# Decoder layers stepped in pairs: two token tiles and two head pairs per cycle instead of one

## What is computed

```python
for i in range(DEPTH):                       # 6
    x = attn_layer(shift_tokens(x), Wqkv[i], q_scale[i], k_scale[i], Wo[i]) + x
    x = ffn_layer(shift_tokens(x), ln_g[i], ln_b[i], W1[i], b1[i], W2[i], b2[i]) + x

def attn_layer(x, Wqkv, qs, ksc, Wo):        # 16 heads of 64
    q, k, v = split heads of x @ Wqkv
    q, k = l2norm(q) * qs, l2norm(k) * ksc   # then both rotated by position
    out = local_attention(q, k, v)           # windows of 32 tokens, each sees itself and the one before
    return out @ Wo

def ffn_layer(x, g, bln, W1, b1, W2, b2):
    a, gate = split((layernorm(x) * g + bln) @ W1 + b1)
    return a * gelu(gate) @ W2 + b2
```

## Time and profile before

| | us |
|---|---|
| median of three runs | 4019.3 (4017.72 to 4019.72) |
| profiled execution | 4023.95 |
| its span, first to last instruction | 4022.2 |
| TensorE busy | 3794.5 (94%) |
| ScalarE busy | 3434.5 (85%) |
| VectorE busy | 3330.3 (83%) |
| GpSimd busy | 2815.3 (70%) |
| mean granted clock of TensorE | 0.983 |

### The profile page before, as it was taken

How to read it: one execution, slowest core, us unless ns; L and a number is a source line. 1 busy time by engine, 2 the same in 40 slices (tenths; PEclk the granted TensorE clock), 3 DMA queues, 4 the chain that set the end, 5 groups by cost and what they waited for, 6 DMA issues and landing times. The chain is left out here.

```text
span 4022.2 us, 139579 instructions
## 1 busy us (share of the span) xinstructions
PE 3794.5 (94%) x47336; PEld 3111.3 (77%) x47336; DVE 3330.3 (83%) x8535; ACT 3434.5 (85%) x11691; POOL 2815.3 (70%) x2443
## 2 busy tenths in 40 slices
PE   7999989999999999999999999999999999999993
PEld 4666668888888888888888888887888888888883
DVE  7888878888888888888878888888888888888883
ACT  7888868888888889888888888889888888888881
POOL 0111178878878787887877878787887878878781
PEclk9999999999999999999999999999999999999996
DMA  2000011111111111111111111111111111111111
GB/s 93 5 17 4 7 30 50 35 27 33 31 48 37 29 32 27 37 50 31 32 28 34 49 33 34 27 33 32 49 36 28 32 27 37 30 30 32 28 27 45
DMA packets 202441, 133.42 MB, mean 33 GB/s; under 512 B 123792, under 2 KB 195856, under 8 KB 200720
## 3 DMA queue, kind: packets, MB, share of 16 engines
q1 hardware_dynamic: 201744, 124.48, 12.0%
HBM read 25.84 MB, written 4.19 MB: 7 GB/s over the span
## 5 line engine op out<-in xcount | busy, mean ns | idle before, releaser
L1050 POOL TENSOR_TENSOR a_rn<-a_ssqc,a_minus_half 128x8 f32<-128x8 f32 x768 | 1273.6, 1658 | 621.7 <-DVE a_ssqc L1170 605.3
L993 ACT ACTIVATE a_E<-bank,a_negmax 128x96 f32<-128x96 f32 x3072 | 1008.1, 351 | 39.3 <-DVE a_negmax L1129 36.6
L1042 POOL TENSOR_TENSOR a_r<-a_u,a_rn 128x512 f32<-128x512 f32 x768 | 809.9, 1055 | 0.7
L1058 POOL TENSOR_TENSOR a_PN<-a_E,a_erec 128x384 f32<-128x384 f32 x768 | 659.0, 858 | 55.1 <-DVE a_erec L1177 55.1
L1020 ACT ACTIVATE a_QK<-bank 128x512 f32<-128x512 f32 x768 | 459.3, 598 | 261.7 <-PE bank L902 260.6
L993 ACT ACTIVATION_READ_ACCUMULATOR a_E<-bank,a_negmax 128x1 f32 x3072 | 669.3, 218 | 0.0
L1129 DVE TENSOR_REDUCE a_negmax<-bank 128x4 f32<-128x384 f32 x768 | 425.5, 554 | 255.8 <-PE bank L919 252.6
L1011 ACT ACTIVATE a_PT<-bank 128x512 f32<-128x512 f32 x768 | 467.6, 609 | 82.2 <-PE bank L892 76.8
L1154 DVE TENSOR_TENSOR a_u<-a_u,a_v 128x512 f32<-128x512 f32 x768 | 523.9, 682 | 6.0 <-issue 1.2
L1147 DVE TENSOR_TENSOR a_v<-bank,a_rot_s 128x512 f32<-128x512 f32 x768 | 524.1, 682 | 0.0
L1140 DVE TENSOR_TENSOR a_u<-bank,a_rot_c 128x512 f32<-128x512 f32 x768 | 522.6, 681 | 0.0
(11 more groups left out here) (139 smaller groups left out, 8701.6 us busy)
## 6 DMA issues: line engine op xcount, KB each, us to landing
a_V_even<-a_V_odd SPq DMA_DIRECT2D x768, 64.0 KB, 1.9
a_V_even<-a_V_odd SPq DMA_DIRECT2D x576, 32.0 KB, 1.9
w_qkv<-in_qkv SPq DMA_DIRECT2D x6, 1536.0 KB, 6.3
a_x_sh<-X SPq DMA_DIRECT2D x48, 128.0 KB
a_f_sh<-X SPq DMA_DIRECT2D x48, 128.0 KB
a_x_sh<-X SPq DMA_DIRECT2D x48, 127.0 KB
a_f_sh<-X SPq DMA_DIRECT2D x48, 127.0 KB
w_out<-in_wo SPq DMA_DIRECT2D x20, 128.0 KB, 2.3
```

Source lines behind the costliest of these rows:

```text
L993: ins = act.activation(E[:, s.par, i, :], p_s[:, i % 2, i // 2 * KW:(i // 2 + 1) * KW], ACT.Exp, bias=negmax[:, s.par, i:i + 1], accum_out ...
L1042: pool.tensor_tensor(heads(r[:, a.par, :]), heads(u[:, a.par, :]), rn[:, a.par, :].unsqueeze(2).to_broadcast([P, 2 * HG, DH]), ALU.mult).t ...
L1050: pool.tensor_tensor(rn[:, a.par, :], ssqc[:, a.par, :], minus_half[:, :], ALU.pow).then_inc(S["rn"], 1)
L1058: pool.tensor_tensor(PN[:, s.par, :, :].rearrange("p i (b k) -> p i b k", b=2)[:, :, :, 0:KW], windows(E[:, s.par, :, :]), windows(erec[:, ...
```

## The change

The layer loop goes over `n` and eight cycles `p` now; a cycle takes two token tiles (`mm` 0 and 1) and both head pairs (`hp` 0 and 1).

- **TensorE**: the tiled matmuls of both head pairs stand one behind the other (16 outputs, then 8 masks, then 16 logits). Projections of the two tiles stand apart, with the rest of the work between them.
- **Joint instructions**: one copy of values and one of outputs for both (512 columns instead of 256), one maximum, one sum of squares, one clamp, one rotation sum (1024 columns), one power (16 columns). Squares, rotation products, exponentials, reciprocals, probabilities and unit scaling stay apart.
- **PSUM**: the logits of both head pairs fill two banks. Transposes go to two banks, `p_ta` and `p_tb`, and the feed-forward results share these two in place of `p_f`.
- **Lags**, in cycles: transposes 2, logits 4, probabilities 6, outputs and output projection 7 (before, in steps: 2, 5, 7, 8, 9).
- **Feed-forward**: still two iterations behind, at other places: statistics in cycle 0, normalisation in 1, turn in 2, gates in 3 and 4, GELU and down projection in 5, values in 6 and 7. The load of `a_f_sh` for batch `n - 2` is issued in cycle 0, the load of the next x in cycle 1.
- **Weights**: the raw query, key and value weights of the next layer are loaded in groups to two buffers (`raw`) instead of whole.

The diff, cut to its core:

```diff
-LAG_T, LAG_S, LAG_PT, LAG_O, LAG_Y = 2, 5, 7, 8, 9
-J_TURN, J_GATE, J_GELU, J_VALUE, J_X = 1, 2, 5, 7, 11
-J_LOAD, J_X_LOAD, J_STATS, J_POWER, J_NORM = 9, 12, 13, 14, 15
+NP = STEPS // 2
+LAG_T, LAG_S, LAG_PT, LAG_O, LAG_Y = 2, 4, 6, 7, 7
+P_BIAS, P_NORM, P_TURN, P_GATE, P_GATES, P_GELU, P_VALUES, P_X = 1, 1, 2, 3, 4, 5, 6, 7
...
         for n in range(NI + 3):
-            for j in range(STEPS):
-                step(n, j)
+            for p in range(NP):
+                cycle(n, p)
...
@@ SyncE @@
+            def move_values(a):
+                name = f"v_moved{a.half}_{a.layer}"
+                m = 2 * a.half
+                sp.wait_ge(S["v_out"], a.k + 1)
+                ge(sp, S[name], moved.get(name, 0))
+                sp.dma_start(V_even[WIN:KW, a.g, m:m + 2, :], V_odd[0:64, a.g, m:m + 2, :]).then_inc(S[name], 16)
...
+            def cycle(n, p):
+                a = pair_at(n, p, 0)
                 if a:
...
+                    move_values(a)
+
+                f = n - 2
+                if p == 0 and 0 <= f < NI:
+                    sp.wait_ge(S["x_out"], f + 1)
+                    ge(sp, S["normed"], f)
+                    shifted_loads(sp, f_sh, X, f % NB, S["f_loaded"])
+                if p == 1 and 1 <= n < NI - 1:
+                    sp.wait_ge(S["xt"], n + 1)
+                    ge(sp, S["f_out"], n + 2 - NB)
+                    shifted_loads(sp, x_sh, X, (n + 1) % NB, S["x_loaded"])
...
@@ TensorE @@
+            def cycle(n, p):
+                project(n, p, 0)
+                transpose_probs(n, p, 1)
+                outputs(n, p)
+                logits(n, p)
+                transpose_qk(n, p, 0)
+                if p == P_BIAS:
+                    shifts(n)
+                if p == P_GATE:
+                    up(n, p, 0, 0, p_tb)
+                if p == P_X and n + 1 < NI:
+                    transpose_x(n + 1)
+                project(n, p, 1)
+                if p == P_TURN:
+                    turn(n)
+                if p == P_GATES:
+                    up(n, p, 1, 0, p_tb)
+                if p == P_VALUES:
+                    up(n, p, 0, 1, p_tb)
+                if p == P_X:
+                    up(n, p, 2, 1, p_ta)
+                values(n, p)
+                if p == P_GATES:
+                    up(n, p, 2, 0, p_ta)
+                if p == P_VALUES:
+                    up(n, p, 1, 1, p_ta)
+                transpose_qk(n, p, 1)
+                output_projection(n, p)
+                transpose_probs(n, p, 0)
+                if p == P_GELU:
+                    down(n)
...
@@ ScalarE @@
+            def cycle(n, p):
+                probs(n, p, 1)
+                outputs(n, p)
+                squares(n, p, 0)
+                queries_and_keys(n, p, 0)
...
+                squares(n, p, 1)
...
+                exps(n, p, 0, 0)
+                exps(n, p, 0, 1)
...
+                queries_and_keys(n, p, 1)
+                values(n, p)
+                probs(n, p, 0)
+                exps(n, p, 1, 0)
+                exps(n, p, 1, 1)
+                if p == P_GELU:
+                    gelu(n)
...
@@ GpSimd @@
+            def cycle(n, p):
+                power(n, p)
+                probs(n, p, 0)
+                probs(n, p, 1)
+                units(n, p, 1)
+                units(n, p, 0)
...
@@ VectorE @@
+            def stats(n):
+                f = n - 2
+                if 0 <= f < NI:
+                    dve.wait_ge(S["f_loaded"], 48 * (f + 1))
+                    statistics(dve, f_sh, st, ag, ve, S["stats"], S["aggr"], S["var"], f)
...
+            def cycle(n, p):
+                if p == P_X:
+                    residual(n)
+                maxima(n, p)
...
+                cosines(n, p, 0)
...
+                sines(n, p, 0)
+                norms(n, p)
+                if p == P_BIAS:
+                    split_up(n)
+                    biases(n)
+                cosines(n, p, 1)
+                clamp(n, p)
+                sines(n, p, 1)
+                if p == P_NORM:
+                    norm(n)
+                reciprocals(n, p, 0)
+                if p == 0:
+                    stats(n)
+                if p == P_GELU:
+                    feed_forward_out(n)
+                reciprocals(n, p, 1)
+                add(n, p)
+                split_qkv(n, p)
```

More of the change, by code:

```diff
@@ L786, in feed_forward, with up @@
+            def up(n, p, c, part, bank):
                 f = n - 2
[L787 to L793 removed]
@@ new lines, in outputs @@
+            def outputs(n, p):
+                a, o = pair_at(n, p, 0), pair_at(n, p, LAG_O)
+                if o:
+                    group = o.group - o.layer * NB * G
+                    pe.wait_ge(S["pt_out0"], o.k + 1)
+                    pe.wait_ge(S["pt_out1"], o.k + 1)
+                    pe.wait_ge(S[f"v_moved{o.half}_{o.layer}"], (group + 1) * 32)
+                    if o.half:
+                        pe.wait_ge(S[f"v_moved0_{o.layer}"], (group + 1) * 32)
+                    pe.wait_ge(S["v_out"], a.k if a else NI * NP)
+                    ge(pe, S["o_out"], o.k)
+                    for hp in range(2):
@@ L922, in logits, with output_projection @@
                                                 skip_group_check=True)
-                        ins.then_inc(S["logits"], 1)
-                for stage in (project, transpose_probs, outputs, logits, transpose_qk, values, output_projection):
-                    stage()
-                feed_forward(n, j)
+                    ins.then_inc(S["logits"], 1)
+            def output_projection(n, p):
+                y = pair_at(n, p, LAG_Y)
+                if y:
+                    pe.wait_ge(S["o_out"], y.k + 1)
+                    if y.pos == 0:
+                        ge(pe, S["x_out"], y.batch)
+                    if y.first and y.half == 0:
+                        ge(pe, S["wo"], 16 * (G * (y.layer - 1) + y.g + 1))
+                    for mm in range(2):
+                        i = 2 * y.half + mm
+                        for hp in range(2):
+                            ins = pe.matmul(p_y[:, i * P:(i + 1) * P], OT[:, y.par, hp, mm * P:(mm + 1) * P],
+                                            w.out[:, 2 * y.g + hp, :], start=(y.pos + hp == 0 and i == 0),
+                                            stop=(y.g == G - 1 and hp == 1), skip_group_check=True)
+                    ins.then_inc(S["y"], 1)
@@ L929, in _ @@
             transpose_x(0)
-            every_iteration(pe, step)
+            every_iteration(pe, cycle)
         @block.scalar
@@ L1192, in _ @@
-            low_x(0)
-            every_iteration(dve, step)
-LAYER_SEMS = ("xt xh xl x_loaded f_loaded qk_out pt_out v_out o_out o y pn pt exp logits r qkt sq qk v max red u u_rot rec rn v_rot "
-              "summed x_out weights w_hi w_lo qkv wo w1 w2 w1_hi w1_lo shift biased rot normed turned f_xh f_xl up gate gelu h "
-              "down f_out var rstd stats aggr").split() + [f"v_moved{i}_{layer}" for i in range(2) for layer in range(DEPTH)]
+                    low_weights(dve, A, raw[:, g % 2, :], g).then_inc(S["w_lo"], 1)
@@ new lines, in add @@
+            def add(n, p):
+                a = pair_at(n, p, 0)
+                if a:
+                    dve.wait_ge(S["u_rot"], 2 * a.k + 2)
+                    dve.wait_ge(S["v_rot1"], a.k + 1)
+                    dve.tensor_tensor(u[:, a.par, :], u[:, a.par, :], v[:, :], ALU.add).then_inc(S["u"], 1)
+                    if n % NB == NB - 1 and a.layer + 1 < DEPTH and a.g == G - 1:
+                        dve.wait_ge(S["scales"], 16 * (a.layer + 1))
+                        for mm in range(2):
+                            rotation(dve, A, w, 2 * a.half + mm).then_inc(S["rot"], 1)
@@ new lines, in _ @@
+            low_x(0)
+            every_iteration(dve, cycle)
+LAYER_SEMS = ("xt xh xl x_loaded f_loaded qk_out0 qk_out1 pt0 pt1 pt_out0 pt_out1 v_out o_out o y pn0 pn1 exp0 exp1 logits r0 r1 "
+              "qkt0 qkt1 sq0 sq1 qk v max red u u_rot rec0 rec1 rn v_rot0 v_rot1 summed x_out weights w_hi w_lo raw0 raw1 scales "
+              "wo w1 w2 w1_hi w1_lo shift biased rot normed turned f_xh f_xl up gate gelu h down f_out var rstd stats "
+              "aggr").split() + [f"v_moved{i}_{layer}" for i in range(2) for layer in range(DEPTH)]
```

824 lines of the change are left out of this document (425 added, 399 removed).

## The result

The changed kernel takes 4368.38 us in the median of four runs (4362.38 to 4371.49), the kernel before beside it 4018.57: a ratio of 1.087 (95% interval 1.085 to 1.089). It is slower by 350 us; 4355 was forecast, in a range of 4160 to 4510.

A forecast was written before the change was run, and what follows sets the result against it. TensorE was taken as the bound; an ordinary iteration would go from 70.5 to 77.7 us (65.5 + 9.65 wait + 2.5 clock), +331 over 46, +338 with the rest: 4355 us, range 4160 to 4510.

The forecast's parts named there:

- The diagnosis: Shift load issued in cycle 0 comes late for VectorE's statistics, so TensorE waits 9.65 us before projecting for cycle 2.
- The pair: On TensorE two steps joined lose 0.35 us once instead of twice: 7.20 us instead of 2 x 3.76.
- The clock: After TensorE's idle stretch it runs at half clock for a while, costing 2.5 us per iteration (1.7 to 3.4).
- The joint operations: Joint instructions on ScalarE, VectorE and GpSimd stay below TensorE's 7.20 us per pair, so their savings are worth nothing.
- rival (1): The pair gains nothing on TensorE because of ScalarE's chain, and the load wait comes on top: 4475 us, chance 0.17.
- The rest: Terms outside the ordinary iterations: second iteration -3.5, fill -2, layer boundaries +8, drain +5 us.
- The second iteration: The iteration without a feed-forward part falls from 61.54 to 58.0 us: -3.5.
- The fill: The start of the layer phase, ahead of the ordinary iterations, changes by -2 us.
- The drain: At the layer phase's end the first statistics also wait, with less queued behind them: +5 us.
- The layer boundaries: At five boundaries TensorE's transposes wait for the bias step in cycle 1, behind the delayed VectorE: +8 us.
- (2): The shift load is short when the queue is empty, so the wait is 2.9 us: about 4000 us, chance 0.07.
- (3): The load is issued early enough and there is no wait: about 3780 us, clearly faster, chance 0.08.

The follow-up runs named there:

- small_tile: early_load with one small 64 by 64 tile matmul added in seven cycles of eight on TensorE: 3909.28 us, against 3843.20 with a whole-array matmul there.
- early_load: The changed kernel with the feed-forward shift load issued in cycle 7 of the iteration before instead of cycle 0: 3813.99 us, ratio 0.949.
- early_split: early_load with the 127-partition DMA of the shifted loads also split into 112 and 15 partitions: 3807.23 us, ratio 0.948.
- bias_first: early_split with VectorE adding the next layer's biases ahead of the sum of squares and the weight split in cycle 1: 3792.51 us, ratio 0.944.
- apart: early_load with the joint copies, maxima, sums, rotated sum and power each as two half instructions: 3836.85 us, against 3819.93 for early_load repeated.

## Why the prediction was right

*The diagnosis.* The bound, the stage and the place of the wait were as put: the value copy 7.7 us into the iteration (measured 7.62), the load at 8.97 (8.83), 10.18 from issue to statistics (10.08), the projection at 24.05 (23.85). The wait was 9.65 by the sum and is 16.92 - 7.13 = 9.8. By its own terms the sum has a slip of 0.07: 7.70 + 1.20 is 8.90, not 8.97.

*The pair.* 7.20 was taken, 7.12 to 7.13 came out. The 0.06 held back for a new change of mode was not spent. Of the 0.35 us lost per step, small_tile confirms about 0.20. The iteration without the wait was put at 65.5; early_load has 65.71.

*The clock.* 2.5 was taken, within 1.7 to 3.4. Cycle 2 is 2.0 us longer on average; of that 1.5 is the clock, which is below the prediction's lowest bound, and 0.4 backlog, which it had put at under 0.3. The mechanism was right and its price too high by 1.0 us; the backlog, and 0.35 us too little in the other terms of the iteration, hide most of that (77.7 forecast, 77.55 measured).

*The joint operations* were put at nothing and are worth 0.45%, in part for the reason that rival (1) gave. The power's price was bounded by 1.66 and 3.3, and is 2.90 us for 16 columns:

```profile
L1157 POOL TENSOR_TENSOR a_rn<-a_ssqc,a_minus_half 128x16 f32<-128x16 f32 x376 | 1090.2, 2899 | 605.5 <-DVE a_ssqc L1316 600.3
```

*The rest* had sizes wrong with opposite signs. The second iteration gave 4.0 for 3.5. The fill was put at -2 and came to -7 (first iteration 49.4 us against 56.7): I had charged the longer lags and not the cheaper cycles. The drain was put at +5 and cost about +15 (early_split's, with hardly a wait for the load, still costs 6.5 more than the drain before). The layer boundaries were put at +8 and cost about 17. That is not the delay from the load, as the prediction had it: an iteration that prepares a layer takes 3.6 us more than an ordinary one in the changed kernel and 4.2 in early_load, where nobody waits for the load, against 1.3 before. Some 12 of the 17 us are the place of the bias step in cycle 1 itself, which bias_first undid; the other 5 lie in the ten iterations next to a boundary and were not traced. The ordinary iterations brought 46 x 7.05 = 324 instead of 331. The first attention happened to be 3 us shorter. In sum +343 on the span against +338: a good part of this closeness is errors that cancel, and so luck; by the terms one by one, ±20 us would have been fair.

*The rivals.* (1), no gain in the pair, is refuted by pairs of 7.13 us where it had 7.52; that the chain it named is nearly as long as the pair is shown by apart. (2), a short load, is refuted by the 10.08. (Its working has a slip too: 8.97 + 2.1 + 1.9 is 13.0, not 12.4, so it stood for about 4030 us and not 4000.) (3), 3780 us without the wait, is refuted too, since the wait is there; but its time is near to what early_load became, 3814: the loss was the price of an order, not of the pairing.

## What to carry to other kernels

When work is regrouped, list for every queue what is issued now, at which time in the new cycle, and how long its result takes; a DMA that was four steps early is easily behind its user after a change that never mentions it. Price the DMA where nobody hides it (the drain showed it) and add the chain behind it. A slowdown of this kind can hide a real gain: undo the suspected place alone before the regrouping is given up.

## What the runs showed of the hardware

- The three DMAs of a shifted load, one of them over 127 partitions in 256-byte pieces, take 10.1 us to their user and keep the queue 8 us, at 18 GB/s for most of it; with the 127 cut into 112 and 15, it is 4.2 and 3.2. The first number was in the drain's rows; that its cause is the count of partitions was not.
- The clock was down behind an idle stretch of 2.3 us as well as behind one of 9.8 (0.81 and 0.76 as the mean of the cycle that follows). Behind one of 5.7 us it was 0.50 for the 3.2 us looked at. Filling the idle stretch with work on zeros kept it at 1.00, and gave back 1.5 of 2.0 us.
- A plain f32 matmul of 128 columns on the whole array showed as two passes of 0.112 us; a transpose of the same size as one of 0.109.
- From whole-array work to a 64-wide tile and back cost 0.19 to 0.23 us.
- GpSimd's power took 2.90 us for 16 columns and 1.66 for 8, which makes an estimated 0.155 us a column with 0.42 before the first.
